# A six-stage decoder: retrieval half passes taken two at a time, and the block mask written by the matrix engine

## The reference, cut to what matters

```python
def _L0_ffn_ref(hidden, W_up, b_up, W_down, b_down, W_q, keys, down_embed, up_embed):
    h = silu(hidden @ W_up.T + b_up) @ W_down.T + b_down          # 128 features
    q = (h @ W_q.T).reshape(b, t, 2, 8, 64)
    sim = einsum('pbthn,hkpn->pbthk', q, keys)                    # 2 sides, 8 heads, 45 keys
    scores, idx = top_k(sim, 8)
    all_scores = sx[..., :, None] + sy[..., None, :]              # 8 x 8 per head
    sc, pk = top_k(all_scores, 8)
    z = einsum('btd,bthkd->bthk', h, down_embed[indices])
    z = silu(z * softmax(sc))
    out = einsum('bthk,bthkd->btd', z, up_embed[indices])

def _L1_attn_ref(x, ...):                                         # causal convolution, then 8 heads
    scores = where(causal, einsum('bqhk,bshk->bhqs', qh * scale, kh), -1e9)   # per block of 16
    attn = softmax(scores); ctx = einsum('bhqs,bshk->bqhk', attn, vh)
    out = (einsum('bqhk,hko->bqo', ctx, wo) + bo) @ proj_w + proj_b

x = x + _L0_ffn_ref(layernorm(x), ...)
x = x + _L1_attn_ref(layernorm(x), ...)
```

## Time and profile before

| | us |
|---|---|
| median of three runs | 1160.37 |
| lowest and highest | 1157.77, 1161.32 |
| the profiled execution | 1160.59 |
| its span in the trace | 1159.0 |
| retrieval stage with its preparation, about | 208 to 583 |
| block attention behind the convolution, about | 637 to 711 |

### The profile page before, as it was taken

How to read it: one execution, slowest core, us unless ns; L and a number is a source line. 1 busy time by engine, 2 the same in 40 slices (tenths; PEclk the granted TensorE clock), 3 DMA queues, 4 the chain that set the end, 5 groups by cost and what they waited for, 6 DMA issues and landing times. The chain is left out here.

```text
span 1159.0 us, 13028 instructions
## 1 busy us (share of the span) xinstructions
PE 840.3 (72%) x4490; PEld 556.9 (48%) x4513; DVE 782.7 (68%) x1296; ACT 490.5 (42%) x703; POOL 547.7 (47%) x394
## 2 busy tenths in 40 slices
PE   5678989767678678677778477956667676569990
PEld 2343744356566566566632464532333343447760
DVE  4764220499999999999624684849999997424442
ACT  2212022454654654554411231368888886112220
POOL 2116000689879879879210223017777775150005
PEclk9768989878788788788879787986876776579995
DMA  3010030000000000000020004906999887033114
GB/s 127 1 73 0 1 115 1 1 1 1 1 1 0 1 1 1 1 1 1 1 96 0 1 1 173 292 17 128 178 186 171 175 165 163 2 110 127 55 59 123
DMA packets 155442, 73.84 MB, mean 64 GB/s; under 512 B 138813, under 2 KB 151297, under 8 KB 154178
## 3 DMA queue, kind: packets, MB, share of 16 engines
q1 hardware_dynamic: 153842, 68.81, 24.2%
q0 software_dynamic: 1536, 4.20, 1.2%
HBM read 27.90 MB, written 11.53 MB: 34 GB/s over the span
## 5 line engine op out<-in xcount | busy, mean ns | idle before, releaser
L680 POOL TENSOR_TENSOR r_pairs<-r_side_exp 128x1035 f32<-128x1035 f32 x128 | 248.3, 1972 | 9.5 <-DVE r_w L845 8.4
L735 PE MATMUL r_head_sum<-ident,r_w 128*128 128x128 f32 (+1 forms) x1024 | 154.3, 316 | 86.4 <-ACT r_w L763 63.0
L763 ACT ACTIVATE r_w<-r_w,r_scale 128x1001 f32<-128x1001 f32 (+1 forms) x128 | 144.4, 1139 | 163.4 <-DVE r_w L845 141.7
L735 PEld LDWEIGHTS r_head_sum<-ident,r_w 128*128 128x128 f32 (+1 forms) x1024 | 141.1, 168 | 107.3 <-ACT r_w L763 81.2
L1529 ACT ACTIVATE c_probs<-c_scores,c_bias,c_q_scale 128x1024 int16<-128x1024 f32 x128 | 154.2, 1205 | 34.9 <-DVE c_bias L1542 26.2
L1540 DVE TENSOR_REDUCE c_neg_max<-c_scores 128x1 f32<-128x1024 f32 x128 | 155.5, 1215 | 13.6 <-PE c_scores L1480 13.4
L1467 POOL CAST c_rounded<-c_probs 128x1024 bf16<-128x1024 int16 x128 | 132.2, 1041 | 47.8 <-ACT c_probs L1529 45.7
L837 DVE SCALAR_TENSOR_TENSOR r_chosen<-r_pairs,r_kept,r_z 128x1024 f32<-128x1024 f32 (+1 forms) x112 | 141.3, 1275 | 12.5 <-ACT r_sims L747 4.3
L1480 PE MATMUL c_scores<-c_kT,c_placed 128*128 128x512 bf16 x233 | 98.2, 507 | 62.7 <-ACT c_probs L1529 54.8
L845 DVE TENSOR_TENSOR r_w<-r_pairs,r_chosen 128x1024 f32<-128x1024 f32 (+1 forms) x112 | 134.8, 1204 | 0.0
L711 PE MATMUL r_head_sum<-r_up,r_wT 128*128 128x256 f32 (+1 forms) x256 | 74.7, 463 | 13.4 <-ACT r_wT L774 13.4
(11 more groups left out here) (271 smaller groups left out, 1415.4 us busy)
## 6 DMA issues: line engine op xcount, KB each, us to landing
ew_w<-in_w SPq DMA_DIRECT2D x2, 2992.0 KB, 13.2
sorted_rows<-ew_w SPq DMA_DIRECT2D x1, 4096.0 KB, 39.1
e_row<-sorted_rows SPq DMA_DIRECT2D x8, 512.0 KB, 8.1
expert_rows<-e_made SPq DMA_DIRECT2D x8, 512.0 KB, 2.9
ew_w<-in_w_near SPq DMA_DIRECT2D x1, 2176.0 KB, 22.2
ctxT<-in_ctxT SPq DMA_DIRECT2D x2, 1024.0 KB, 8.6
r_up<-in_up SPq DMA_DIRECT2D x1, 2048.0 KB, 9.7
c_pT<-c_rounded SPq DMA_TRANSPOSE x128, 2.8
```

Of the source, the lines that this page charges most:

```text
L680: nc.gpsimd.tensor_tensor(pairs[:, v % MADE, :].rearrange("p (a b) -> p a b", b=KEYS), a.broadcast_to([P, ROWS, KEYS]), b.broadcast_to([P, ...
L735: last = nc.tensor.matmul(head_sum[0:m, b // 4, (b % 4) * P:(b % 4 + 1) * P], w[:, v % RING, b * P:b * P + m], ident[:, :], start=(h == 0 ...
L763: nc.scalar.activation(w[:, v % RING, 0:COLS[f]], w[:, v % RING, 0:COLS[f]], ACT.Silu, scale=scale[:, t % 2, h:h + 1]).then_inc(silu_done, 1)
```

## The change

In retrieval:

- VectorE takes the half passes in pairs: pick, pick, weigh, weigh. A weigh no longer belongs to the half pass before.
- The 8 x 8 grid is made by GpSimd (`best_grid`), under two new semaphores, and VectorE starts `best_pairs` with the MAX.
- `best_keys(t + 1)` is called right behind `best_pairs(t)`, at the start of f = 0, and `residual(t - 1)` behind the pair of heads 6 and 7 of f = 0.
- MADE goes from 8 to 12. GpSimd weighs heads 4 and 5, seven half passes behind its products; `below_best` and `exps` move to the start of f = 1.

In block attention:

- The mask is bf16. Two matmuls with a bf16 identity write it to the score banks, and the scores are added to it there.
- VectorE takes negated maxima from PSUM and nothing else before the exp. ScalarE takes eight exps of 128 columns from PSUM, one per head with that head's maximum as bias, into three buffers instead of two.
- TensorE's `join` stands ahead of the next scores, and VectorE's residual is cut in two around the maxima.

```diff
-        MADE, RING = 8, 14
+        MADE, RING = 12, 14
-        BY_POOL, LEAD = (2, 5), 4
-        BELOW_AT, EXP_AT, SUM_AT, ADD_AT, PROJECT_AT = 7, 3, 0, 5, 5
+        BY_POOL, LEAD = (4, 5), 7
+        BELOW_AT, EXP_AT, SUM_AT, ADD_AT, PROJECT_AT = 0, 0, 0, 7, 5
...
+            def best_grid(t):
+                pool.wait_ge(exps_ready, t + 1)
+                if t >= 1:
+                    pool.wait_ge(kept_ready, t)
...
+                nc.gpsimd.tensor_tensor(grid[:, :, :].rearrange("p h (a b) -> p h a b", b=TOP), a, b, ALU.mult).then_inc(grid_ready, 1)
...
                 if f == 0 and h == 0:
-                    pool.wait_ge(exps_ready, t + 1)
+                    best_grid(t)
...
             best_keys(0)
-            for v in range(PARTS_R):
+            for v in range(0, PARTS_R, 2):
                 k, t, f, h = place(v)
                 if h == 0 and f == 0:
                     best_pairs(t)
-                if h == 0 and f == 1 and t + 1 < NT:
-                    best_keys(t + 1)
+                    if t + 1 < NT:
+                        best_keys(t + 1)
...
                 pick(v)
-                if v >= 1 and not by_pool(v - 1):
-                    weigh(v - 1)
-                if f == 0 and h == ADD_AT and t >= 1:
+                pick(v + 1)
+                for n in (v, v + 1):
+                    if not by_pool(n):
+                        weigh(n)
+                if f == 0 and h + 1 == ADD_AT and t >= 1:
                     residual(t - 1)
-            weigh(PARTS_R - 1)
             residual(NT - 1)
...
                 if t >= 2:
-                    pe.wait_ge(masked, t - 1)
+                    pe.wait_ge(exp_done, t - 1)
+                for j in range(2):
+                    nc.tensor.matmul(scores[:, t % 2, j, :], s.identb[:, :],
+                                     s.mask[:, :].rearrange("p (o n) -> p o n", o=1).broadcast_to([P, CB, P]),
+                                     start=True, stop=False, skip_group_check=True)
...
+                for n in range(HEADS_B):
+                    last = nc.scalar.activation(p[:, t % PROBS, n, :], scores[:, t % 2, n // CB, (n % CB) * P:(n % CB + 1) * P],
+                                                ACT.Exp, bias=neg_max[:, t % 2, n:n + 1])
...
+                nc.vector.tensor_reduce(neg_max[:, t % 2, :], scores[:, t % 2, :, :].rearrange("p j (c n) -> p (j c) n", n=P),
+                                        AX.X, ALU.max, negate=True).then_inc(max_ready, 1)
```

More of the change, by code:

```diff
@@ L806, in best_pairs @@
             def best_pairs(t):
[L808 removed]
+                dve.wait_ge(grid_ready, t + 1)
                 if t >= 2:
                     dve.wait_ge(silu_done, 2 * HEADS_R * (t - 1))
[L811 to L813 removed]
                 for h in range(HEADS_R):
                     last = nc.vector.max(kept[:, t % 2, h, :], grid[:, h, :])
[L816 removed]
+                last.then_inc(kept_ready, 1)
+                dve.wait_ge(kept_ready, t + 1)
                 chain.step(nc.vector.tensor_reduce(scale[:, t % 2, :], kept[:, t % 2, :, :], AX.X, ALU.add))
@@ L892, in block_attention @@
         s.proj = sb("proj", [WIDTH + 1, D])
-        s.mask = sb("mask", [P, P])
+        s.mask, s.identb = sb("mask", [P, P], BF16), sb("identb", [P, P], BF16)
+        s.mask_ready = sem("mask_ready")
         s.loaded = sem("out_loaded")
@@ L1059, in turn @@
                 for n in range(HEADS_B):
[L1060 removed]
+                    last = nc.tensor.transpose(turned[:, n // CB, (n % CB) * P:(n % CB + 1) * P], p[:, t % PROBS, n, :], ident[:, :])
                 last.then_inc(turned_ready, 1)
@@ L1103, in exps @@
             def exps(t):
-                act.wait_ge(shifted, t + 1)
-                nc.scalar.activation(p[:, t % 2, :, :], p[:, t % 2, :, :], ACT.Exp).then_inc(exp_done, 1)
+                act.wait_ge(max_ready, t + 1)
+                if t >= PROBS:
+                    act.wait_ge(turned_ready, t - PROBS + 1)
+                for n in range(HEADS_B):
+                    last = nc.scalar.activation(p[:, t % PROBS, n, :], scores[:, t % 2, n // CB, (n % CB) * P:(n % CB + 1) * P],
+                                                ACT.Exp, bias=neg_max[:, t % 2, n:n + 1])
+                last.then_inc(exp_done, 1)
             exps(0)
@@ L1120, in _, with maxima, residual_a @@
             chain = sh.chain.on(dve)
[L1122 removed]
+            def maxima(t):
                 dve.wait_ge(scored, t + 1)
[L1125 to L1134 removed]
+                nc.vector.tensor_reduce(neg_max[:, t % 2, :], scores[:, t % 2, :, :].rearrange("p j (c n) -> p (j c) n", n=P),
+                                        AX.X, ALU.max, negate=True).then_inc(max_ready, 1)
             def sums(t):
                 dve.wait_ge(exp_done, t + 1)
[L1138 removed]
+                if t >= 2:
+                    dve.wait_ge(probs_ready, t - 1)
+                chain.step(nc.vector.tensor_reduce(row_sum[:, t % 2, :], p[:, t % PROBS, :, :], AX.X, ALU.add))
                 nc.vector.reciprocal(row_sum[:, t % 2, :], row_sum[:, t % 2, :]).then_inc(sum_ready, 1)
[L1141 removed]
+            def residual_a(t):
                 dve.wait_ge(joined_ready, t + 1)
@@ L1150, in _ @@
             dve.wait_ge(s.loaded, 48)
-            prepare(0)
-            prepare(1)
+            maxima(0)
+            maxima(1)
             sums(0)
@@ L1156, in _ @@
                     sums(t + 1)
+                if t >= 1:
+                    residual_a(t - 1)
                 if t + 2 < NT:
-                    prepare(t + 2)
+                    maxima(t + 2)
                 if t >= 1:
-                    residual(t - 1)
-            residual(NT - 1)
+                    residual_b(t - 1)
+            residual_a(NT - 1)
+            residual_b(NT - 1)
 HEADS_C = 16
```

40 lines of the change are left out of this document (18 added, 22 removed).

## The result

The changed kernel takes **1166.7 us** (median of six runs, 1163.6 to 1167.9), the kernel before 1159.7 beside it (six runs): a ratio of 1.0057, 95% interval 1.0042 to 1.0073. The forecast was 1166.5. The profiled run took 1167.6 us with a span of 1166.0.

A forecast was written before the change was run, and what follows sets the result against it. The prediction took VectorE to set retrieval's pace, one tile each 44.2 us. From 1160.6 us, retrieval's +18.0 and block attention's -12.0 gave 1166.6, say 1166.5, with a range of 1150 to 1180.

The forecast's parts named there:

- The detour residual, transposes, `z`, pick: Retrieval, between the halves: f = 1's first pick waits for `z` behind forty transposes behind the residual, 6.84 us at full clock.
- The clock's share: Retrieval: TensorE pauses about 4 us before the transposes and restarts at a lower clock, 2.3 us a tile, bounds 0 to 6.2.
- Rival A: Retrieval: TensorE's clock holds through the pause, 16 us less, 1150.5 us in all; chance 0.20.
- rival C: Retrieval: the clock stays at 1.2 GHz through the whole detour, 27 us more, 1194 us in all; chance 0.07.
- A tile: Retrieval: a tile, counted between the ends of last weighs, takes 47.1 us against 44.2 before.
- Rival B: Retrieval: the detour doesn't bind as `z` comes in time, tiles of 39.0 us, 1108 us in all; chance 0.08.
- First tile: Retrieval's first tile: picks start at 222.18, no residual, 1.6 us of wait ahead of f = 1, end at 258.4.
- Behind the last weigh: Retrieval's end: by the order of GpSimd's weighing four silus queue, and the last ends about 1.1 us later than before.
- Retrieval: The whole retrieval stage: 18.0 us slower, +16.9 by the last weigh's end and about 1.1 behind it.
- Block attention: The whole block attention stage: 12.0 us faster, between -15 and -7, first transposes 3.2 us sooner, tiles 5.8 us.
- Rival D: Block attention gains nothing: TensorE at half clock needs about 9 us a tile; 1178.5 us in all; chance 0.12.
- The eight exps: Block attention: ScalarE's eight exps of 128 columns take 2.3 us, between 1.1 and 3.0.

The follow-up runs named there:

- z_first: The changed kernel with TensorE's projections of the second half put ahead of the forty transposes: 1108.2 us, ratio 0.957 to the kernel before.
- add_at5: The changed kernel with the residual one pair earlier, behind heads 4 and 5 of f = 0: 1119.7 us, ratio 0.966 to the kernel before.
- filler: The changed kernel with 22 unused matmuls a tile on TensorE between the up projections and the transposes: 1148.1 us, ratio 0.991 to the kernel before.
- lead4: The changed kernel with GpSimd weighing heads 4 and 5 four half passes behind its products, not seven: 1162.1 us, ratio 1.0045 to the kernel before.
- retr_only: The changed kernel's retrieval with the block attention of before: 1182.4 us, ratio 1.020 to the kernel before.
- attn_only: The kernel before with the change's block attention alone: 1141.3 us, ratio 0.985 to the kernel before.
- attn_order: The kernel before with the new block attention but the old order in a tile, masks and maxima kept new: 1141.5 us, ratio 0.986.
- keys_mid: The changed kernel with the next tile's maxima back ahead of f = 1's first pick, subtraction and exponentials four half passes later: 1236.1 us, ratio 1.068.

## Why the prediction was right, step by step

- **The detour residual, transposes, `z`, pick**: right in mechanism (`z_first`, `add_at5`), 9.6 us against 9.14 in the tile shown.
- **The clock's share**: 2.3 us was taken, 2.4 measured by the waits of `filler` (16.7 / 7); the forty transposes took 6.2 to 7.5 us (6.5 to 7 forecast) against 4.6. The row from which the 2.3 was taken had a pause of 2.4 us ahead of it and not one of 4, so that it came so near is in part luck. Rival A, that it holds, is out; rival C too, since it was back at 384 to 385, as the forty transposes ended.
- **A tile**: forecast 47.1 us, measured 46.7 to 47.7 from one start of the forty transposes to the next. The seven waits for `z`, 7.6 to 8.9 us, are those forecast (7 to 9), and the pairs are as forecast. No residual between tiles waits; the MAX of `kept` waited once, 4.0 us for the grid in the first tile, where the picks wait for the similarities behind it. Rival B is out by these waits.
- **First tile**: the wait ahead of f = 1 was 1.54 us (1.6 forecast) and the tile ended at 258.1 (258.4). **Missed** is what followed: 3.5 us for `z` ahead of the second. I had looked for what stands behind GpSimd's weighs only in the last tile; in the first the products ahead of them cost as well.
- **Behind the last weigh**: 1.1 us more was taken, 2.0 measured (12.22 against 10.20). `lead4` shows that it is not the lead. `filler` weighs the same heads and waits 10.84: so 1.4 of the 2.0 go with the clock (24 transposes take 4.51 us and not 3.14), a cost that the prediction had nowhere behind the last weigh, and 0.6 are left for the order of the weighs, for which 1.1 was taken.
- **Retrieval**: +18.0 forecast, +24.1 by the last residual's start, +23.7 by `retr_only`. Of the missing 6 us, 3.5 are the first tile and 0.9 the end. The rest, 1.7, was not taken apart; the detour is longer than forecast in the middle tiles (9.6 against 9.14).
- **GpSimd's grid**: 1.11 us (1.0 forecast), hidden, with 2.3 us of idle time before it (3 to 5 forecast).
- **Block attention**: -12.0 forecast, -16.6 measured by `attn_only`, past my bound of -15. Rival D, no gain, is out. First transposes 3.7 us sooner within the stage (3.2). The mis-sized terms are the tiles, 5.5 us (the last group of transposes starts at 709.0, so 38.6 / 7) against 5.8, and the 1.5 us for a cold start, of which the tiles show nothing (the first eight transposes took 1.97 us and not 1.09, but the second group follows after 5.1): 2.0 and 1.5, and 0.5 at the start, together 4.0 of the 4.6. The chain that I added up returned after two tiles with the joining in it; it measured 11.0 against the 11.4 of the sum. `attn_order` shows that taking the joining out of the scores' way is worth 0.2 us in two tiles of the trace, and nothing in the times.
- **The eight exps** took 2.18 us, one 393 ns; I took 2.3. The Trainium skill's figure ("ScalarE: Activation LUTs", What ACT_TABLE_LOAD costs) gave an estimate of 2.4; the trace's 2.18 is 0.2 below it.

The total was met because two errors cancelled: retrieval costs 6 us more than forecast, and block attention gains 4.6 more. The signs and the order of the terms were right; the fit to 0.2 us is luck.

## What to carry to other kernels

A pass taken off the busiest engine was here worth only what the next engine's queue order let through. Before batching work in pairs, ask for each step that moved which queue holds its consumer's input, and put short producers that another engine waits for (here `z`, 1.84 us) ahead of long ones. Where TensorE pauses some 4 us between batches, as here, count its restart at the lower clock (2.4 us a tile here), and try one step earlier before anything else. When an edit puts one step later, look which other steps it moves with it: `keys_mid` moved two things, and its result can't be put down to one of them.

## What the runs showed of the hardware

- A pause of 3.9 us behind 10 us of matmuls ended at half clock (0.50, 1.2 GHz), and forty f32 transposes took 7.24 us; behind a pause of 2.0 us (`add_at5`) they took 4.56, at full clock. Behind one of 2.3 us (`z_first`) the clock was at 0.50 a microsecond into the new work, and `z` took 3.52 us where it took 1.84. Matmuls whose result is unused, put into the pause, made the kernel 17 to 18.6 us faster.
- GpSimd's product of two broadcast operands took 1.11 us for 512 elements a partition, and VectorE's 2.47 for the same in seven tiles. In the first tile VectorE's took 0.69. The prediction says that GpSimd stood still then; by the trace it stood still up to 215.55, and the grid ran from 215.51, so the two overlap, and GpSimd's product took 2.46 us where such products take 1.95 (median).
- Sixteen maxima of 45 columns took 1.8 us together, though each has a duration of 193 ns: a sum of mean durations overstates such a run.
